# Another order for the first tile of a gated cross-attention and MLP kernel

## The reference

```python
x = x + tanh(g_xattn) * attention(layernorm(x), ctx, ctx)   # 16 heads of 32, 77 context rows, biases
x = x + tanh(g_ffn) * ffn(layernorm(x))                     # two linear layers, inputs and weights rounded to 127 steps per tensor
```

## Time and profile before

| | us |
|---|---|
| median of 3 runs | 580.91 |
| the profiled execution | 581.38 |
| its span | 579.6 |
| TensorE busy | 565.7 (98%) |
| VectorE busy | 442.1 (76%) |
| ScalarE busy | 336.6 (58%) |
| GpSimd busy | 300.8 (52%) |

### The profile page before, as it was taken

How to read it: one execution, slowest core, us unless ns; L and a number is a source line. 1 busy time by engine, 2 the same in 40 slices (tenths; PEclk the granted TensorE clock), 3 DMA queues, 4 the chain that set the end, 5 groups by cost and what they waited for, 6 DMA issues and landing times. The chain is left out here.

```text
span 579.6 us, 9118 instructions
## 1 busy us (share of the span) xinstructions
PE 565.7 (98%) x3272; PEld 321.6 (55%) x3272; DVE 442.1 (76%) x622; ACT 336.6 (58%) x408; POOL 300.8 (52%) x242
## 2 busy tenths in 40 slices
PE   6999999999999999999999989999999999999997
PEld 3834746567476575674765854444444544444443
DVE  4698986979878698695895778788887799835282
ACT  3355374763855737438247538777786696555350
POOL 5457565762763666716072429655507247503383
PEclk9999999999999999999999999999999999999999
DMA  8966000411503305111001169987778995979766
GB/s 310 384 280 219 1 2 0 155 65 31 185 4 110 110 0 183 37 37 75 0 1 74 72 217 336 368 325 278 284 278 327 368 320 217 340 297 390 228 235 218
DMA packets 41944, 106.62 MB, mean 184 GB/s; under 512 B 3377, under 2 KB 4145, under 8 KB 37297
## 3 DMA queue, kind: packets, MB, share of 16 engines
q1 hardware_dynamic: 39952, 103.70, 48.8%
q10 hardware_dynamic: 1952, 2.42, 1.2%
HBM read 64.16 MB, written 41.94 MB: 183 GB/s over the span
## 5 line engine op out<-in xcount | busy, mean ns | idle before, releaser
L1552 PE MATMUL ps<-h_sb,w_q 128*128 (+1 forms) x488 | 109.7, 379 | 0.1
L1851 PE MATMUL ps<-w_q,h_q 128*128 128x512 bf16 x448 | 96.9, 379 | 0.0
L1934 POOL TENSOR_TENSOR xo<-xo,b2s 128x512 f32<-128x512 f32 x32 | 52.5, 1672 | 70.4 <-DMA xo<-x_dram 52.4
L1552 PEld LDWEIGHTS ps<-h_sb,w_q 128*128 128x128 bf16 x488 | 46.7, 98 | 52.2 <-issue 1.1
L1851 PEld LDWEIGHTS ps<-w_q,h_q 128*128 128x128 bf16 x448 | 43.8, 98 | 52.9
L1619 ACT ACTIVATE xo<-ps,b1s,sc 128x1024 f32<-128x1024 f32 x48 | 57.6, 1205 | 20.0 <-PE ps L1552 16.7
L794 ACT ACTIVATE prob<-ps 77x1024 f32<-77x1024 f32 x64 | 61.7, 1013 | 10.6 <-PE ps L521 10.6
L1705 DVE TENSOR_REDUCE hmax<-xo 128x1024 f32 (+1 forms) x48 | 58.3, 1217 | 12.1 <-ACT xo L1619 11.4
L1738 POOL TENSOR_SCALAR y<-x,mean,rs 128x512 f32<-128x512 f32 x24 | 50.2, 2098 | 29.6 <-DVE xq L1686 23.2
L780 ACT ACTIVATE q_hi<-ps,bq_sb 128x512 fp32r<-128x512 f32 x32 | 22.0, 688 | 63.8 <-DVE ps L999 63.6
L1286 POOL TENSOR_TENSOR c_lo<-c_sb,c_hi 128x512 fp32r<-128x512 f32 x28 | 38.4, 1391 | 34.6 <-ACT c_hi L822 34.6
(11 more groups left out here) (194 smaller groups left out, 1110.5 us busy)
## 6 DMA issues: line engine op xcount, KB each, us to landing
h_dram<-xo SPq DMA_DIRECT2D x48, 512.0 KB, 2.9
h_sb<-h_dram SPq DMA_DIRECT2D x16, 1024.0 KB, 11.2
x_dram<-x SPq DMA_DIRECT2D x8, 1024.0 KB, 3.9
xo<-x_dram SPq DMA_DIRECT2D x8, 1024.0 KB, 5.0
x<-h_dram SPq DMA_DIRECT2D x8, 1024.0 KB, 7.8
x<-in_x SPq DMA_DIRECT2D x7, 1024.0 KB, 7.1
out<-xo SPq DMA_DIRECT2D x7, 1024.0 KB, 8.5
xr<-in_x_t SPq DMA_DIRECT2D x24, 256.0 KB, 3.7
```

Of the source, the lines that this page charges most:

```text
L1552: mm = nc.tensor.matmul(ps[:, 2 * (m % 2) + s, :], w1_q[:, k, m * P:(m + 1) * P], xq_t[:, one(2 * j + s), k, :], start=(k == 0), stop=(k = ...
L1851: mm = nc.tensor.matmul(ps[:, 4 * s + t, :], h_q[s][:, m, t * P:(t + 1) * P], w2_q[:, m, :], start=(m == 0), stop=(m == MF - 1))
L1934: nc.gpsimd.tensor_tensor(xo[:, s, t, :], xo[:, s, t, :], b2s[:], ALU.add).then_inc(xb_on, 1)
```

## The change

1. Loads. SP issues Wq pieces 0, 2 and 3, both halves of Wk, x^T pieces 0 and 2, then the identity and the x tiles. ScalarE's queue has Wq piece 1, the context, x^T pieces 1 and 3, the two biases and the x tiles. Context and halves of Wk get semaphores of their own.
2. TensorE: seven small products at the start (`warm_up`), the weight means, then all keys, then the query products. The ten idle turns go. In piece 0 the terms go in the order hi x hi for all groups, wq_lo, xt_lo. The row turn moves ahead of group 1's third piece, and its bank is 3.
3. VectorE: statistics and keys ahead of the low parts 2 and 3 of Wq; `pick` last.
4. GpSimd: the fourth `xt_low` behind the power, with a wait for it, and the keys' low parts behind both.
5. ScalarE: a small copy first, Wq's pieces one ahead of those of x^T, the key casts ahead of the row's copy, the third `q_high` ahead of the gate, and `c_copy(0, 1)` ahead of two conversions of the next chunk.

```diff
--- before.py
+++ after.py
@@ -194,2 +194,4 @@
         k_in = sem("k_in")
+        ctx_in = sem("ctx_in")
+        wk_in = [sem(f"wk_in{s}") for s in range(2)]
         wq_in = [sem(f"wq_in{k}") for k in range(KD)]
@@ -285,3 +287,3 @@
 
-        MEAN_BANK, ROW0_BANK = 3, 2
+        MEAN_BANK, ROW0_BANK = 3, 3
 
@@ -358,8 +360,9 @@
 
-                for k in (0, 2):
+                for k in (0, 2, 3):
                     sp.dma_start(wq_raw[:, k, :], slices(wq_t)[:, k, :]).then_inc(wq_in[k], 16)
-                sp.dma_start(sh.ident[:], eye).then_inc(ident_in, 16)
+                for s in range(2):
+                    sp.dma_start(wk_raw[:, 2 * s:2 * s + 2, :], slices(wk_t)[:, 2 * s:2 * s + 2, :]).then_inc(wk_in[s], 16)
                 for k in (0, 2):
                     sp.dma_start(xt0_raw[:, k, :], xt_v[k, 0]).then_inc(xt0_in[k], 16)
-                sp.dma_start(wk_raw[:, 0:2, :], slices(wk_t)[:, 0:2, :]).then_inc(k_in, 16)
+                sp.dma_start(sh.ident[:], eye).then_inc(ident_in, 16)
                 for t in (0, 2):
@@ -425,16 +428,25 @@
 
-                def first_q(m, ks):
+                def warm_up():
+
+                    pe.wait_ge(mean_w_on, 1)
+                    for _ in range(7):
+                        nc.tensor.matmul(ps[:, BS, 0:P], mean_w[:].to_broadcast([P, P]),
+                                         mean_w[:].to_broadcast([P, P]), start=True, stop=True)
+
+                HH, HL, LH = (wq_hi, xt_hi), (wq_hi, xt_lo), (wq_lo, xt_hi)
+
+                def first_q(m, ks, terms=(HH, LH, HL)):
 
                     for k in ks:
-                        for w, r in ((wq_hi, xt_hi), (wq_hi, xt_lo), (wq_lo, xt_hi)):
-                            if m == 0 and r is xt_hi and w is wq_hi:
+                        for term in terms:
+                            w, r = term
+                            if m == 0 and term is HH:
                                 pe.wait_ge(wc_hi_on, k + 1)
                                 pe.wait_ge(xt_hi_on, k + 1)
-                            if m == 0 and r is xt_lo:
+                            if m == 0 and term is HL:
                                 pe.wait_ge(xt_lo_on, k + 1)
-                            if m == 0 and w is wq_lo:
+                            if m == 0 and term is LH:
                                 pe.wait_ge(wc_lo_on, k + 1)
                             mm = nc.tensor.matmul(ps[:, q_bank(0, m), :], w[:, k, m * P:(m + 1) * P], r[:, k, :],
-                                                  start=(k == 0 and w is wq_hi and r is xt_hi),
-                                                  stop=(k == KD - 1 and w is wq_lo))
+                                                  start=(k == 0 and term is HH), stop=(k == KD - 1 and term is HL))
                     if KD - 1 in ks:
@@ -592,7 +604,13 @@
 
-                def project_k(m):
-                    pe.wait_ge(k_in, 80)
-                    bank, at = divmod(m, 3)
+                def project_k():
+
+                    pe.wait_ge(ctx_in, 16)
                     for k in range(KD):
-                        mm = nc.tensor.matmul(ps[:, bank, at * B * NK:(at + 1) * B * NK], wk_raw[:, k, m * P:(m + 1) * P],
+                        if k % 2 == 0:
+                            pe.wait_ge(wk_in[k // 2], 16)
+                        for m in range(GROUPS - 1):
+                            nc.tensor.matmul(ps[:, m, 0:B * NK], wk_raw[:, k, m * P:(m + 1) * P], ctx_sb[:, k, :],
+                                             start=(k == 0), stop=(k == KD - 1))
+                    for k in range(KD):
+                        mm = nc.tensor.matmul(ps[:, 0, B * NK:2 * B * NK], wk_raw[:, k, (GROUPS - 1) * P:GROUPS * P],
                                               ctx_sb[:, k, :], start=(k == 0), stop=(k == KD - 1))
@@ -603,11 +621,13 @@
                 def first_step():
-                    for k in range(2):
+                    for term in (HH, LH, HL):
                         for m in range(KD):
-                            first_q(m, [k])
+                            first_q(m, [0], (term,))
+                    for m in range(KD):
+                        first_q(m, [1])
                     first_q(0, [2])
-                    for m in range(GROUPS):
-                        project_k(m)
-                    first_q(0, [3])
+                    pe.wait_ge(ident_in, 16)
                     row_turn(0)
-                    first_q(1, [2, 3])
+                    first_q(1, [2])
+                    first_q(0, [3])
+                    first_q(1, [3])
                     first_q(2, [2, 3])
@@ -725,5 +745,5 @@
 
+                warm_up()
                 weight_means()
-                pe.wait_ge(ident_in, 16)
-                idle_turns(nc, sh, BS, 10)
+                project_k()
                 first_step()
@@ -837,9 +857,12 @@
                 def first_step():
-                    for k in range(KD):
-                        xt_high(0, k)
+                    centred_high(0)
+                    for k in range(1, KD):
                         centred_high(k)
-                    row_copy(0)
+                        xt_high(0, k - 1)
+                    xt_high(0, KD - 1)
                     split_k(0)
+                    row_copy(0)
                     q_high(0, 0)
                     q_high(0, 1)
+                    q_high(0, 2)
                     act.wait_ge(wo_in, 64)
@@ -847,3 +870,2 @@
                     nc.scalar.copy(wo_hi[:, 0, :], wo_raw[:, 0, :]).then_inc(w_hi_on, 1)
-                    q_high(0, 2)
                     nc.scalar.copy(wo_hi[:, 1, :], wo_raw[:, 1, :]).then_inc(w_hi_on, 1)
@@ -863,5 +885,5 @@
                     exponentials(0, 5)
+                    c_copy(0, 1)
                     xt_high(1, 2)
                     xt_high(1, 3)
-                    c_copy(0, 1)
                     exponentials(0, 6)
@@ -944,4 +966,4 @@
 
-                for k in (1, 3):
-                    nc.scalar.dma_start(wq_raw[:, k, :], slices(wq_t)[:, k, :]).then_inc(wq_in[k], 16)
+                nc.scalar.dma_start(wq_raw[:, 1, :], slices(wq_t)[:, 1, :]).then_inc(wq_in[1], 16)
+                nc.scalar.dma_start(ctx_sb, slices(ctx_t)).then_inc(ctx_in, 16)
                 for k in (1, 3):
@@ -950,6 +972,6 @@
                 nc.scalar.dma_start(sh.bq[:], bq).then_inc(k_in, 16)
-                nc.scalar.dma_start(ctx_sb, slices(ctx_t)).then_inc(k_in, 16)
-                nc.scalar.dma_start(wk_raw[:, 2:4, :], slices(wk_t)[:, 2:4, :]).then_inc(k_in, 16)
                 for t in (1, 3):
                     nc.scalar.dma_start(x1[:, t, :], x_v[0][:, t, :]).then_inc(x0_in[t], 16)
+                act.wait_ge(half_set, 2)
+                nc.scalar.copy(ve2[:], minus_half[:])
                 first_step()
@@ -1216,6 +1238,2 @@
                 nc.vector.memset(v[64:P, :, :], 0.0).then_inc(v_padded, 1)
-                dve.wait_ge(ident_in, 16)
-                for r in range(4):
-                    q = slice(DK * r, DK * (r + 1))
-                    nc.vector.tensor_copy(sh.pick[q, :], sh.ident[q, DK * r:DK * r + GROUPS]).then_inc(idents_on, 1)
                 centre_wq(0)
@@ -1226,4 +1244,2 @@
                 centre_wq(3)
-                centred_low(2)
-                centred_low(3)
                 for t in range(TT):
@@ -1232,8 +1248,14 @@
                     first_mean(t)
-                dve.wait_ge(k_in, 80)
-                dve.wait_ge(k_mm, GROUPS)
+                dve.wait_ge(k_in, 32)
+                dve.wait_ge(k_mm, 1)
                 for m in range(GROUPS):
-                    bank, at = divmod(m, 3)
+                    bank, at = (m, 0) if m < GROUPS - 1 else (0, 1)
                     nc.vector.tensor_scalar(k_t[:, m, :], ps[:, bank, at * B * NK:(at + 1) * B * NK], bk_sb[:, m:m + 1], float(DK) ** -0.5,
                                             ALU.add, ALU.mult).then_inc(k_biased, 1)
+                centred_low(2)
+                centred_low(3)
+                dve.wait_ge(ident_in, 16)
+                for r in range(4):
+                    q = slice(DK * r, DK * (r + 1))
+                    nc.vector.tensor_copy(sh.pick[q, :], sh.ident[q, DK * r:DK * r + GROUPS]).then_inc(idents_on, 1)
                 first_step()
@@ -1307,2 +1329,4 @@
                         pool.wait_ge(s_mm, PAIRS * (NC // B))
+                    else:
+                        pool.wait_ge(ln1_rstd, rstd_value(0))
                     src = sh.k_t1[:, :, :] if b else k_t[:, :, 0:NK]
@@ -1323,5 +1347,8 @@
                 def first_step():
-                    for k in range(KD):
+                    for k in range(KD - 1):
                         xt_low(0, k)
                     rstd_1(0)
+                    pool.wait_ge(ln1_rstd, rstd_value(0))
+                    xt_low(0, KD - 1)
+                    pool.wait_ge(xt_lo_on, KD)
                     split_k(0)
```

(23 more changed lines are left out.)

## The result

| | before | with the change |
|---|---|---|
| median of 7 runs, us | 580.96 (580.64 to 581.77) | 578.59 (577.87 to 580.21) |
| the profiled execution / its span | 581.38 / 579.6 | 580.21 / 578.4 |

The ratio is 0.9963 with a 95% interval of 0.995 to 0.9976: 2.1 us less, between 1.4 and 2.9 (the two medians differ by 2.4). The forecast was 3.3 us less, 577.6, in a range of 576.4 to 580.0. The seven runs fall into two groups: four from 577.87 to 578.59 with a mean granted clock of 0.999 or 1.000, and three from 579.71 to 580.21 with 0.996 or 0.997. The profiled execution is of the upper group.

What follows compares the result with a forecast made beforehand. TensorE, busy 565.7 of 579.6 us, was taken as the bound, with gains in the head and one later wait. 2.3 + 1.0 = 3.3 us less than the 580.91 median gave 577.6 us, range 576.4 to 580.0.

Steps and rivals of the forecast that it cites:

- rival D: TensorE idling from 9.6 to 10.9 us drops to 1.2 GHz: plus 2.0 us, 579.6 us; chance 0.04.
- The landings: Head transfers: context near 8.0 us, Wk's halves 8.0 and 10.9, last x^T pieces 11.6 and 12.4, x tiles 15.4.
- The last low part: VectorE in the head: low part 3 of Wq ends at 21.8 us, delayed by waits for GpSimd's x^T part.
- The casts of pick: VectorE in the head: four small casts end at 22.5 us, after which scaling starts instead of at 24.01.
- The copy: First tile's end: c_sb copied before two x^T conversions removes TensorE's 0.99 us wait; 1.0 us, bounds 0 and 1.0.
- Rival B: Only the head counts; the 0.99 us reappears as a wait for x^T piece 3: 578.6 us; chance 0.10.
- the two terms: The head's gain, 2.3 us at the first maximum, and the moved c_sb copy's 1.0 us at the tile's end.
- Rival F: Second half of Wk lands late in the head, at 17.05 us, making the kernel slower: 583.8 us; chance 0.08.

Runs made afterwards that it cites:

- the wider gap: The change with TensorE waiting for both halves of Wk before any key product, its idle stretch unfilled: 581.89 us, ratio 1.0009.
- filled run: The change with nine more idle TensorE products between weight means and keys: 578.18 us, ratio 0.9946; run once more, 578.85 us, ratio 0.9956.

## Why the prediction was right or wrong

**The direction and the range held**; the size was 3.3 us forecast against 2.1 (1.4 to 2.9) measured. The step that failed is rival D, the clock, which I gave 0.04 and kept out of the sum. Its price was nearly right (2.0 forecast, 1.6 measured), its chance was not: 5 of 19 runs of the change show it by time and clock, and 9 of 12 with the wider gap. I had argued that nothing in the trace shows a fall; but once TensorE had started, the trace of before had no idle stretch longer than 0.99 us, so it couldn't show what a longer one does. The gap was also at another place and longer than worked out: 8.2 to 10.2, ahead of all keys, instead of 9.6 to 10.9 in their middle. The Trainium skill's warning of idle gaps between bursts of matmuls (TensorE: Matmul & The Clock Gate, Why this matters for your kernels) was the better guide here. It warns of longer gaps than the 2.03 us that stood before this fall; the runs decide, with 1.00 falling to 0.50 and 1.6 us lost.

**Without a fall the working comes out at 3.1 us** instead of 3.3 at the next tile's first product (48.35 against 51.47):

| step | forecast | change, no fall | change, with fall |
|---|---|---|---|
| key products start | 8.0 | 10.32 | 10.25 |
| first query products | 13.6 | 14.49 | 16.09 |
| scaling | 22.5 | 22.81 | 24.42 |
| scores | 24.4 | 24.67 | 26.28 |
| maximum | 25.4 | 25.54 | 27.14 |
| power ends | 19.1 | 19.4 | 19.4 |

*The landings* were wrong. The context came at 6.1 instead of 8.0, Wk's halves at 10.1 and 12.0 instead of 8.0 and 10.9, x^T piece 0 at 13.3 instead of 11.6. I had taken turns row by row from one stretch at 11 to 14 us; in the first microseconds the context's short rows went through faster than that, and ScalarE's queue moved on to x^T while SP's still had Wk to do. Of the 2.3 us by which the keys started late only 0.9 reached the first query product, since all sixteen then ran without a gap.

*The last low part* ended at 20.28, not 21.8: VectorE had both in 1.29 us, and it was GpSimd's subtraction that took 1.99 instead of 1.27. VectorE had started at 18.99, GpSimd at 19.46, so the wait fell on GpSimd, the other way round than forecast. *The casts of pick* took 2.35 us instead of 0.74, beside GpSimd's subtractions, so that VectorE's chain ended at 22.5 after all: two errors that cancel, by luck. Nor was this chain the bound, as I had it: the scaling then waits 0.28 us for the last query product, at 22.81. The version with pick moved shows that the casts don't set the time.

*The copy* was forecast at 1.0 us and gives 0.9 in the trace of the copy alone, 0.6 to 2.2 by its runs. Rival B falls. At the next tile's first product the two terms add up to the 3.1 us: 2.15 at the maximum and the wait of 0.99. But they are not independent: with the head changed and the copy not moved that wait is 0.33 and the next tile already starts 2.6 us earlier (48.90 against 51.47), so in the traces some of the copy's 1.0 us comes with the head.

*Rival F* was right in kind: with the keys 1.5 us later, the undisturbed runs are 1.8 us slower than those of the change, and with its falls of the clock level with the kernel before (1.0009).

*What stays open:* by the trace the undisturbed change is 3.1 us ahead, by medians (578.25 for its ten undisturbed runs against 580.84) 2.6. The profiled execution of the kernel before, 581.38 us, lies 0.5 above that median, and the one of the change, 577.95, lies 0.3 below its own, so the pair shows more than the medians do. Part may be that the kernel before has its wait of 0.99 us in the profiled execution and a shorter one in others, as the version without the moved copy has 0.33; that was not tried. The gain at 461 us is the one at 48 us in every profile (462.60, 461.13, 459.46), so it is not lost in between.

## What to carry to other kernels

When loads are put in front of TensorE's first real work, look at how long it will idle between its warm-up and that work. A few products into an unused bank cost nothing that these runs can tell (578.18 against 578.25 for the undisturbed runs of the change), and with the wide gap they kept the clock in all of twelve runs. They should end before the awaited input lands: eighteen ran some 0.65 us past it. Work moved ahead of everything must be priced by the landing of its last input, since nothing covers it (2.16 us later here, 2.11 us lost); its worth is read on the other engines, in what they no longer do at the moment when everything is late together.

## What was not expected of the hardware

- TensorE's clock fell from 1.00 to 0.50 in the middle of the key products, at about 11.0 us, when the idle stretch (8.2 to 10.2 us) was already over, and stayed there to about 14.4 us. The same program kept a mean clock of 0.998 or more in 14 of 19 runs, and a version with as long a gap (2.01 us) kept it in its profiled execution.
- A second place where it can fall lies at 338 us, seen in the profile of one filled run; its trace reaches `output` 0.95 us later behind the same point than another one without it (460.75 - 48.69 against 459.49 - 48.38).
- Four casts of 32 x 4 elements on VectorE took 2.35 us beside GpSimd's subtractions and 0.73 without them.
